# Low parts of weights on GpSimd placed at set points of VectorE's work, and one order of work on VectorE, in a fused attention and feed-forward kernel

## The reference

```python
x = x + tanh(g_xattn[0]) * xattn(layernorm(x), ctx, Wq, Wk, Wv, Wo, ...)   # 32 heads, 8 key/value heads, 256 keys
x = x + tanh(g_ffn[0])   * ffn(layernorm(x), w_gate, w_up, w_down)         # inner width 1376, int8 cuts
x = x + tanh(g_xattn[1]) * softmax(ctx @ layernorm(x).T / 128**0.5) @ ctx  # in outline
x = x + tanh(g_ffn[1])   * moe(layernorm(x), ...)                          # 16 experts, 2 per token, shared part
```

## Time and profile before

| | |
|---|---|
| median of 3 runs | 1199.65 us (1199.49 to 1199.93) |
| profiled execution, time | 1198.55 us |
| its span in the trace | 1196.8 us |
| TensorE matmul busy | 1176.8 us (98%) |
| VectorE busy | 830.3 us (69%) |
| ScalarE busy | 580.5 us (49%) |
| GpSimd busy | 326.9 us (27%) |

### The profile page before, as it was taken

The page is one execution under the profiler, slowest core; times in us unless marked ns, Lnnn a source line. Parts: engine busy times, 40 slices in busy tenths (PEclk is TensorE's granted clock), DMA queues, the critical chain, the costliest instruction groups (busy, mean ns, idle before and its releaser), DMA issues.

```text
span 1196.8 us, 20842 instructions
## 1 busy us (share of the span) xinstructions
PE 1176.8 (98%) x6979; PEld 1008.7 (84%) x6979; DVE 830.3 (69%) x2402; ACT 580.5 (49%) x1352; POOL 326.9 (27%) x286
## 2 busy tenths in 40 slices
PE   8999999999999999999999999999999999999998
PEld 7888888888888888888988888888787777778786
DVE  6867677666766766667666667668877887875355
ACT  5645455454545455454554545554444445543432
POOL 4513022221303212031231203122342412225542
PEclk9999999999999999999999999999999999999999
DMA  7001010000101010010000000002122212583316
GB/s 281 12 25 54 1 37 18 36 33 2 53 0 35 18 35 35 0 53 0 35 19 33 35 0 0 1 1 56 32 80 79 81 54 71 204 321 100 108 44 246
DMA packets 36266, 69.65 MB, mean 58 GB/s; under 512 B 5858, under 2 KB 22242, under 8 KB 34166
## 3 DMA queue, kind: packets, MB, share of 16 engines
q1 hardware_dynamic: 30726, 56.65, 13.7%
q0 software_dynamic: 3760, 8.40, 2.2%
q10 hardware_dynamic: 1728, 3.93, 0.8%
HBM read 60.57 MB, written 12.32 MB: 61 GB/s over the span
## 4 chain that ended last, share of the span: by engine, by line
PE 60%; DVE 21%; issue 9%; ACT 5%; POOL 2%; DMA 2%; SPq 1%; DVEq 0%; ACTq 0%; POOLq 0%
PE bank L414 14%; PE bank L416 14%; PE bank L415 14%; PE bank L2274 5%; PE bank L2123 3%; DVE probs L1276 3%; ACT probs L881 2%; PE bank L1951 2%; PE bank L2286 2%; DVE iq L1475 2%; DVE k_junk L1231 2%; DVE row_max L1249 2%; DVE pt_lo L1263 2%; POOL k_rstd L648 1%; PE bank L1893 1%
## 5 line engine op out<-in xcount | busy, mean ns | idle before, releaser
L881 ACT ACTIVATE probs<-bank,exp_bias,q_rstd 128x256 f32<-128x256 f32 x256 | 141.1, 562 | 135.7 <-DVE exp_bias L1257 135.7
L1268 DVE TENSOR_TENSOR o_lo<-bank,o_hi 128x512 fp32r<-128x512 f32 x64 | 44.2, 691 | 175.6 <-ACT o_hi L874 175.6
L414 PE MATMUL bank<-wkv_hi,kv_src_lo 128*128 128x256 f32 x512 | 145.0, 283 | 0.7 <-DVE kv_src_lo L1318 0.7
L416 PE MATMUL bank<-wkv_hi,kv_src_hi 128*128 128x256 f32 x512 | 145.0, 283 | 0.0
L415 PE MATMUL bank<-wkv_lo,kv_src_hi 128*128 128x256 f32 x512 | 144.9, 283 | 0.0
L652 POOL TENSOR_TENSOR q_rstd<-q_var,minus_half 128x8 f32<-128x8 f32 x32 | 52.4, 1637 | 299.0 <-DVE q_var L1236 299.0
L870 ACT ACTIVATE pt_hi<-bank 128x512 fp32r<-128x512 f32 x128 | 69.6, 596 | 116.1 <-PE bank L1951 114.4
L414 PE MATMUL bank<-wo_hi,o_lo 128*128 128x512 f32 x256 | 104.2, 407 | 1.6 <-DVE o_lo L1268 1.2
L414 PE MATMUL bank<-wq_hi,kv_src_lo 128*128 128x512 f32 x256 | 103.2, 403 | 0.6 <-DVE k_lo L1218 0.6
L416 PE MATMUL bank<-wo_hi,o_hi 128*128 128x512 f32 x256 | 101.5, 396 | 0.0
L415 PE MATMUL bank<-wo_lo,o_hi 128*128 128x512 f32 x256 | 101.0, 394 | 0.0
(11 more groups left out here) (300 smaller groups left out, 3079.2 us busy)
## 6 DMA issues: line engine op xcount, KB each, us to landing
weights<-r_w SPq DMA_DIRECT2D x16, 768.0 KB, 9.7
wq_raw<-wq SPq DMA_DIRECT2D x8, 1024.0 KB, 4.8
wo_raw<-wo SPq DMA_DIRECT2D x8, 1024.0 KB, 4.8
wkv_raw<-wkv SPq DMA_DIRECT2D x8, 512.0 KB, 3.3
gu_raw<-w_gate SPq DMA_DIRECT2D x10, 256.0 KB, 3.4
gu_raw<-w_up SPq DMA_DIRECT2D x10, 256.0 KB, 3.7
wd_raw<-w_down SPq DMA_DIRECT2D x10, 256.0 KB, 3.8
y_back<-y_dram SPq DMA_DIRECT2D x5, 512.0 KB, 9.0
```

What stands on the lines that cost most here:

```text
L414: eng.matmul(out_ap, a_lo, b_hi, start=start, stop=False)
L416: return eng.matmul(out_ap, a_hi, b_hi, start=False, stop=stop)
L881: act.activation(probs[:, h, :], scores_ps[h // 2][:, (h % 2) * 256:(h % 2) * 256 + 256], ACT.Exp, bias=exp_bias[:, h:h + 1], scale=q_rstd ...
L1268: dve.tensor_tensor(o_lo[:, par, :], o_ps[:, :], o_hi[:, par, :].bitcast(F32), ALU.subtract)\
```

## The change

Five edits.

- ScalarE runs `wkv_high(g + 1)` ahead of the exponentials of tile 5, not behind `o_high`.
- GpSimd's `wkv_low(g + 1)` waits for the bias of tile 5 too (`bias_ready` at g*8 + 6).
- GpSimd's low part of gate and up weights is made in two instructions of 128 x 512, each with its own count, so `gu_lo_ready` counts two for a chunk. The first piece waits for iq of the chunk before (`iq_ready` at 2c), the second for the clip of this chunk's first half (`inter_step` at 8c + 1), and wd_lo for iq of the first half (`iq_ready` at 2c + 1).
- In SP's chunk loads the wait for `gu_lo_ready` inside the loop is dropped; the one for wd_lo stays. The other counts are doubled.
- In the first group's second tile VectorE runs `maxima` and `bias_of` ahead of `k_low`, `pt_low` ahead of `low_pair(3)`, and `o_low` behind `q_low`.

```diff
@@ -531,10 +531,9 @@
             with sp.Fori(1, (CH - 1) // 2) as i:
                 for j in range(2):
                     c = i * 2 + j
-                    sp.wait_ge(gu_lo_ready, c - 1)
                     sp.wait_ge(wd_lo_ready, c - 1)
                     load_chunk(c, j, P)
-            sp.wait_ge(gu_lo_ready, CH - 2)
+            sp.wait_ge(gu_lo_ready, 2 * (CH - 2))
             sp.wait_ge(wd_lo_ready, CH - 2)
             load_chunk(CH - 1, 0, TAIL)

@@ -551,7 +550,7 @@

             load_context(0)
             load_context(1)
-            sp.wait_ge(gu_lo_ready, CH)
+            sp.wait_ge(gu_lo_ready, 2 * CH)
             sp.wait_ge(wd_lo_ready, CH)
             for e in range(SHARED):
                 sp.dma_start(s_raw[:, e, :], s_w[e, :, :]).then_inc(s_loaded, 16)
@@ -688,6 +687,7 @@
                     if before_end(g, b, 2) and not (isinstance(g, int) and g == 0 and b == 0):
                         k_root(next_pair)
                     if b == 4 and before_end(g, b, 4):
+                        pool.wait_ge(bias_ready, g * NB + 6)
                         wkv_low(g + 1)
                     if before_end(g, b, 2):
                         q_root(next_pair, (b // 2 + 1) % 2)
@@ -695,12 +695,10 @@
             groups(pool, one_group)


-            def gu_low(c, j, width):
+            def gu_low(c, j, i, width):
                 pool.wait_ge(gu_hi_ready, c + 1)
-                pool.tensor_tensor(gu_lo[:, j, :, :, 0:width].rearrange("p a c n -> p (a c) n"),
-                                   gu_raw[:, j, :, :, 0:width].rearrange("p a c n -> p (a c) n"),
-                                   gu_hi[:, j, :, :, 0:width].bitcast(F32).rearrange("p a c n -> p (a c) n"),
-                                   ALU.subtract).then_inc(gu_lo_ready, 1)
+                pool.tensor_tensor(gu_lo[:, j, i, :, 0:width], gu_raw[:, j, i, :, 0:width],
+                                   gu_hi[:, j, i, :, 0:width].bitcast(F32), ALU.subtract).then_inc(gu_lo_ready, 1)

             def wd_low(c, j, width):
                 pool.wait_ge(wd_hi_ready, c + 1)
@@ -711,13 +709,19 @@

             def next_low(c, j, width, following):
                 if following:
-                    gu_low(c + 1, 1 - j, following)
+                    if after_first(c):
+                        pool.wait_ge(iq_ready, c * 2)
+                    gu_low(c + 1, 1 - j, 0, following)
+                    pool.wait_ge(inter_step, c * 8 + 1)
+                    gu_low(c + 1, 1 - j, 1, following)
+                    pool.wait_ge(iq_ready, c * 2 + 1)
                     wd_low(c + 1, 1 - j, following)

             for t in range(3):
                 ln_root(NB + t)
             pool.wait_ge(probs_ready, 4 * (G * NB - 1))
-            gu_low(0, 0, P)
+            gu_low(0, 0, 0, P)
+            gu_low(0, 0, 1, P)
             routing_maps()
             for t in range(3, NB):
                 ln_root(NB + t)
@@ -939,13 +943,13 @@
                     if isinstance(g, int) and g == 0 and b == 1:
                         key_source_high(6)
                         key_source_high(7)
+                    if b == 5 and before_end(g, b, 3):
+                        wkv_high(g + 1)
                     exps(n, b)
                     if isinstance(g, int) and g == 0 and b == 1:
                         q_copy(next_pair)
                     if prev:
                         o_high(n - 1, (b - 1) % 2)
-                    if b == 5 and before_end(g, b, 3):
-                        wkv_high(g + 1)
                     if b % 2 == 0 and before_end(g, b, 2):
                         for half in range(2):
                             kv_high(next_pair, half, par)
@@ -1350,16 +1354,16 @@
                     if after_start(g, b, 3):
                         add_y(n - 3, (b - 3) % NB)
                     if isinstance(g, int) and g == 0 and b == 1:
-                        k_low(next_pair, par)
                         maxima(n)
                         bias_of(n, b)
+                        k_low(next_pair, par)
+                        pt_low(n - 1)
                         low_pair(3)
-                        pt_low(n - 1)
                         normalise(n)
                         q_norm(next_pair)
-                        o_low(n - 1, (b - 1) % 2)
                         for half in range(2):
                             q_low(next_pair, half, par)
+                        o_low(n - 1, (b - 1) % 2)
                         continue
                     maxima(n)
                     if after_start(g, b, 1):
@@ -2074,7 +2078,7 @@

             def inner_chunk(c, j, width, following):
                 if after_first(c):
-                    pe.wait_ge(gu_lo_ready, c + 1)
+                    pe.wait_ge(gu_lo_ready, c * 2 + 2)
                     inner_half(c, j, width, 0)
                 else:
                     pe.wait_ge(ln_lo_ready[0], 2 * NB)
@@ -2104,6 +2108,7 @@
             turn_x(5)
             inner_part_of(0, 0, P, 0, 0, 1, KC)
             turn_x(6)
+            pe.wait_ge(gu_lo_ready, 2)
             inner_part_of(0, 0, P, 0, 1, 0, 1)
             turn_x(7)
             inner_part_of(0, 0, P, 0, 1, 1, KC)
```

## The result

| us | before | changed kernel |
|---|---|---|
| median of the runs made side by side | 1199.57 (1198.79 to 1199.93) | 1189.3 (1189.0 to 1189.74) |
| profiled execution | 1198.55 | 1189.0 |
| its span | 1196.8 | 1187.2 |

The ratio is 0.9913, 95% interval 0.9897 to 0.9928: faster by 0.9%. The forecast was 1189.6. The changed kernel was run a second time, beside a kernel before at 1198.66: 1188.42 (1187.84 to 1188.55), ratio 0.9915 [0.9901, 0.9928].

The account below looks back on a forecast made before the run. TensorE, busy 1176.8 of 1196.8 us, bounds the kernel, so only its standstills can be won. 6.2 + 1.2 + 2.9 - 0.2 = 10.1 us takes the median from 1199.65 to 1189.6; part bounds give 1188.8 to 1193.3, extended 0.5 lower.

Parts of the forecast that it names:

- Part 1: Groups, tile 5, seven times: wkv_low behind the bias and wkv_high ahead of exponentials free probs; 6.2 us gained.
- Part 2: First pair: maxima first delays k_lo by 0.77 us but brings the scores forward; 1.2 us gained, bounds 0.5 to 1.6.
- Part 3: Inner chunks: three timed pieces bring VectorE's chain to 10.68 us, under TensorE's 10.88; 2.9 us gained, bounds 1.0 to 2.9.
- The price of the waits: Inner chunks: GpSimd's three new waits compare with numbers from registers; 0 to 0.1 us taken for each.
- rival A: Inner chain stays the bound at 11.2 us or more, gaining 1 us or nothing; 1191.5, up to 1192.5; chance 0.19.
- The narrow place at chunk 2: Inner chunks: gu_lo's second piece ends at 875.86, TensorE starts the chunk at 876.18; 0.3 us to spare.
- Part 4: First inner chunk: low part in two pieces takes longer than in one; cost 0.2 us, bounds 0 and 0.5.
- The stages behind: Down projections, routing and experts, after the changed stages: they follow TensorE and keep their length.
- B: Group part lands by half: GpSimd late or ScalarE's 1.81 us not free, wkv_lo meets probs again; 1192.7; chance 0.07.
- C: Inner chunks: tr_v is held beside GpSimd after all, chain about 12.3 us, kernel slower at 1203.6; chance 0.03.
- D: Whole change: the new waits are met already and GpSimd's order stays; 1199.6; chance 0.03.
- E: Inner chunks: iq's 2.65 us have another cause than gu_lo, so Part 3 removes nothing; 1192.5; chance 0.03.

Follow-up runs that it names:

- written out: The changed kernel with GpSimd's loop over the inner chunks unrolled, so its waits compare with constants instead of registers; 1187.99 us, ratio 0.9913.

## Why the prediction came out

The time was foretold 0.3 us off, and the kernel before ran at 1199.57 beside it instead of 1199.65, so 10.3 us were gained where 10.1 were forecast. Part by part:

- **Part 1, 6.2 forecast, 6.2 measured**, and lost again when undone. The steps hold too: wkv_lo ends at 197.45 ahead of o_lo, probs start 1.03 us behind it (1.0 said), q_lo has 1.1 us to spare (1.2 said). What the prediction did not see is that GpSimd's new wait does nothing for the time: it treated wait and move as one, and only the move was needed. The spare that it had worked out says why the held bias costs nothing without the wait.
- **Part 2, 1.2 forecast, 1.3 measured.** The second query tile comes 0.75 us later (0.77 said), q_lo directly behind q_var, and q_var has moved forward by 0.72 us once the earlier start is taken off (0.6 said).
- **Part 3, 2.9 forecast, 2.9 measured**, although one term was mis-sized. The chain takes 10.90 us, not 10.68. Held clip and rounding were 0.35 and 0.54 us late (0.37 and 0.51 said), but the second half's clip 0.50 instead of 0.32, because wd_lo starts 0.21 us behind iq, 0.13 of it through register work; written out it is 0.38, and the period 10.69. The price of the waits had been kept apart with 0 to 0.1 us each, and the whole is 0.21, so the sum was inside its own bounds. The reason given for the low price, that GpSimd works out the next number while its subtraction runs, holds for the second piece, whose wait costs nothing; ahead of the other two pieces register work stands behind the wait. At 10.90 the chain is level with TensorE's 10.88, where 10.68 would have left 0.2 us in hand, and rival A was nearer than its size suggests, though it didn't come: no wait for gu_lo, and a chain under 11.2. The prediction also gave the gain to three pieces timed and placed; the split alone gives it. At 11.08 TensorE waits a little, 0.85 us over the whole stage; at 11.85 it costs 6 us. The narrow place at chunk 2 had 0.5 us to spare instead of 0.3.
- **Part 4, -0.2 forecast, -0.1 measured**, within the bounds.
- **The stages behind** were to keep their length, and in the two profiles of the changed kernel the experts are 1.0 and 0.5 us longer. Kernels with the same code there differ by as much, but what makes the difference was not tried and stays open. With it the profiled execution lies 0.5 us above its forecast of 1188.5, since the 0.8 us gained at the start covers only part of the 1.5. That this one execution came so near owes something to two stretches that the sum left at nothing. The medians don't need that luck: the parts as measured add up to 10.3, the medians give 10.3 and 10.2.
- **Rivals.** B, C, D and E are refuted: each group gained 0.8 to 0.9, tr_v beside a subtraction takes 0.69, the order changed, and iq takes 0.69 once no subtraction runs beside it, 1.55 beside a split one and 2.65 beside a whole one. That iq with both inputs in SBUF is held at all speaks for the page "SBUF — State Buffer" of the Trainium skill, section "SBUF: two separate sides", as the prediction read it. That the loser waits for the whole instruction is borne out as well, with instruction taken literally: two instructions queued back to back are not one, iq takes 1.55 us beside them instead of 2.65.

## What to carry to other kernels

When GpSimd subtractions hold VectorE, first ask which of them can be moved to a time in which VectorE waits for something else, and move what *feeds* them; a wait in front of them alone does nothing if their input is the late part. Where they can't be moved, cut them into short instructions: one held operation gets its turn at each boundary. That is worth much where one long hold stood (iq, 2.65 us down to 1.55) and little for a row of short operations (the four scalings, 3.21 us beside two pieces). Cost a hold by what VectorE could have done in that stretch, since a piece that lies beside a gap or beside an operation that reads PSUM is nearly free, while the same piece one step later costs most of its length (0.2 us a chunk in one place, 0.95 us in the other, for a piece of 1.3).

## What the runs showed of the hardware

- A VectorE operation that is held by a GpSimd subtraction of 128x512 ends 0.02 us (exp_bias, 128x4), 0.15 us (a scaling of 128x256), 0.28 us (clip, rounding) or 0.54 us (iq, the fraction) behind that piece, even where the next piece is queued directly behind it (iq 1.55 us; rounding 0.95 and then the fraction 1.66 us).
- The following piece pays for it: 1.48 us instead of 1.29 where a clip or a rounding took its turn at the boundary, 1.74 us where iq did. A piece that started while VectorE's correction ran took longer too: 1.52 us, and 2.62 instead of 2.40 us for the whole subtraction in the kernel before.
- Between the end of iq and GpSimd's subtraction lie 0.08 to 0.09 us where the wait stands on the subtraction itself, and 0.16 and 0.21 us where a register instruction of 0.03 and 0.07 us stands in between.
